# Transformer block with two-of-eight experts on one core: the weight splits of the first sequence spread out, and the experts' bias rows prepared in another way

## What is computed

```python
q, k, v = (xn @ W.T for W in (Wq, Wk, Wv))          # per head
sim = 50 * tanh((q @ k.T) / 8 / 50); sim = where(causal, sim, min)
x = x + (softmax(sim) @ v) @ Wo.T
t = layernorm(x)
shared = gelu(t @ sw1 + sb1) @ sw2 + sb2
probs = softmax(t @ gate_w + gate_b); the two largest -> combine
y[e] = gelu(t @ w1[e] + b1[e]) @ w2[e] + b2[e]
out = x + shared + sum over e of combine[:, e] * y[e]
```

## Time and profile before

| | us |
|---|---|
| median of 3 runs (lowest, highest) | 2082.99 (2081.49, 2083.97) |
| the profiled execution, its own time | 2080.42 |
| its span, first to last instruction | 2078.6 |
| busy: PE, PEld, DVE, ACT, POOL | 1922.9, 1517.5, 1527.5, 1415.6, 1030.0 |

### The profile page before, as it was taken

The page is one execution under the profiler, slowest core; times in us unless marked ns, Lnnn a source line. Parts: engine busy times, 40 slices in busy tenths (PEclk is TensorE's granted clock), DMA queues, the critical chain, the costliest instruction groups (busy, mean ns, idle before and its releaser), DMA issues.

```text
span 2078.6 us, 39943 instructions
## 1 busy us (share of the span) xinstructions
PE 1922.9 (93%) x14653; PEld 1517.5 (73%) x14653; DVE 1527.5 (73%) x2803; ACT 1415.6 (68%) x2170; POOL 1030.0 (50%) x1195
## 2 busy tenths in 40 slices
PE   6799999999999999999999999999999873999998
PEld 4576767676767676767676767676767652999998
DVE  5576878787878787878787878787876885565565
ACT  6677777777777777777777777777777731544444
POOL 3344454545454545454545454545454643444444
PEclk9999999999999999999999999999999995999999
DMA  4000010101010101010101010101010124764664
GB/s 132 1 11 11 11 42 11 42 11 42 11 42 11 42 11 42 11 42 12 41 13 40 14 39 15 38 16 37 16 37 6 37 72 134 232 189 132 196 183 140
DMA packets 73665, 112.51 MB, mean 54 GB/s; under 512 B 9715, under 2 KB 52218, under 8 KB 73476
## 3 DMA queue, kind: packets, MB, share of 16 engines
q1 hardware_dynamic: 58468, 67.86, 11.3%
q0 software_dynamic: 15008, 42.10, 5.4%
HBM read 63.10 MB, written 48.65 MB: 54 GB/s over the span
## 4 chain that ended last, share of the span: by engine, by line
PE 81%; ACT 12%; DVE 5%; issue 2%; DMA 1%; POOL 0%; SPq 0%; POOLq 0%; DVEq 0%
PE bank_o L1239 12%; PE ring L1218 7%; PE ring L1145 6%; PE ring L1151 6%; PE ring L1146 6%; PE ring L1197 6%; PE ring L1223 6%; ACT prob L585 3%; PE acc L1262 3%; PE ring L1204 3%; PE acc L1264 3%; PE acc L1270 3%; ACT prob L591 2%; PE bank_d L1253 2%; PE ring L1404 2%; PE ring L1409 2%
## 5 line engine op out<-in xcount | busy, mean ns | idle before, releaser
L508 POOL TENSOR_SCALAR_AFFINE_SELECT prob<-prob 128x256 f32<-128x256 f32 x512 | 231.1, 473 | 567.7 <-ACT prob L591 567.6
L585 ACT ACTIVATE prob<-ring 128x1024 f32<-128x1024 f32 (+1 forms) x384 | 326.3, 875 | 205.5 <-PE ring L1223 202.3
L591 ACT ACTIVATE prob<-prob 128x1024 f32<-128x1024 f32 (+1 forms) x384 | 342.7, 915 | 5.2
L520 POOL TENSOR_TENSOR key_sum<-prob 128x768 f32<-128x768 f32 x128 | 243.0, 1898 | 205.6 <-PE bank_d L1253 193.9
L1239 PE MATMUL bank_o<-prob,v 128*32 128x512 f32 (+3 forms) x4096 | 306.6, 440 | 25.1 <-DVE weighed L801 14.4
L1218 PE MATMUL ring<-qT,kT 128*128 128x256 f32 (+3 forms) x1024 | 240.2, 336 | 64.7 <-ACT qT L608 20.0
L780 DVE TENSOR_TENSOR kT<-ring,kT 64x512 fp32r<-64x512 f32 x256 | 176.3, 689 | 153.6 <-ACT kT L598 146.8
L1218 PEld LDWEIGHTS ring<-qT,kT 128*128 128x128 f32 x1024 | 166.6, 191 | 146.5 <-issue 71.2
L1239 PEld LDWEIGHTS bank_o<-prob,v 128*32 128x32 f32 x4096 | 118.0, 110 | 185.1 <-issue 159.1
L796 DVE RECIPROCAL norm<-bank_d 128x512 f32<-128x512 f32 x64 | 214.9, 3357 | 21.7 <-PE bank_d L1253 20.1
L1223 PE MATMUL ring<-q_lo,kT 128*128 128x256 f32 (+3 forms) x1024 | 229.6, 326 | 0.9 <-DVE q_lo L785 0.9
(11 more groups left out here) (224 smaller groups left out, 4689.7 us busy)
## 6 DMA issues: line engine op xcount, KB each, us to landing
xin<-first SPq DMA_DIRECT2D x71, 257.0 KB, 3.1
xin<-second SPq DMA_DIRECT2D x71, 129.0 KB, 2.3
xin<-base SPq DMA_DIRECT2D x71, 128.0 KB, 2.5
x_next<-in_x SPq DMA_DIRECT2D x16, 512.0 KB, 4.6
x_res<-in_x SPq DMA_DIRECT2D x16, 512.0 KB, 4.0
raw_e<-in_w SPq DMA_DIRECT2D x4, 1024.0 KB, 6.7
first<-pad SPq DMA_DIRECT2D x9, 257.0 KB, 4.4
second<-pad SPq DMA_DIRECT2D x9, 129.0 KB, 7.5
```

The costliest lines, as they stand in the source:

```text
L508: last = nc.gpsimd.affine_select(out=diag, in_=diag, compare_op=ALU.is_ge, fill=0.0, base=0, pattern=[[0, 2], [1, P]], channel_multiplier=-1)
L520: nc.gpsimd.tensor_tensor(sums[:, :, :], t0[:, :, P:N], t13[:, :, 0:N - P], ALU.add).then_inc(sum_steps, 1)
L585: nc.scalar.activation(probs[p % PROBS][u][:, :, :], slot[:, :, 0:UNIT_COLS[u]], ACT.Tanh, scale=SCALE / SOFTCLAMP).then_inc(act_emptied, 1)
L591: nc.scalar.activation(cols, cols, ACT.Exp, scale=SOFTCLAMP).then_inc(exp_done, 1)
```

## The change

The weight splits of sequence 0 are done at other places and partly on another engine. `w_v` leaves `parts`; POOL makes both of its parts ahead of its loop. Of `w_k` and `w_q` DVE first splits the first 128 columns of each chunk (`split_lo_part`), and the rest after K and Q of pair 0; PE's projection of pair 1 now waits for the rest. `w_o`, `w_1` and `w_2` are split at the end of pairs 2, 3 and 4 (`LATER_SPLIT`), on ACT and on DVE. PE's wait for `w_o` and the constants moves from the end of pair 2 to that of pair 3.

The biases `b1`, `b2` and `sb2` are loaded by one transfer, laid over all 128 partitions (16, 16 and 2 columns each). DVE splits them with two instructions in the opening, and SP, after a wait for them that stands ahead of its loop over the sequences, issues six transfers from SBUF to SBUF that place the high and low parts in their rows. `prepare_bias`, its four loads and the waits for them are gone, as is the work on `sb2` on two partitions. The diff, its repeated declarations left out:

```diff
@@ -177,6 +177,10 @@
         b_rows = sb("b_rows", [P, E * D], F32R)
+        BIAS = E * D // P
+        bias_raw = sb("bias_raw", [P, 2 * BIAS + D // P])
+        bias_part = [sb(f"bias_{s}", [P, 2 * BIAS + D // P], F32R) for s in ("h", "l")]
@@ -322,7 +326,7 @@
         loaded = [sem(f"loaded{k}") for k in range(len(loads))]
-        parts = [("w_k", 0), ("w_q", 1), ("w_v", 2), ("w_o", 3), ("w_1", 5), ("w_2", 6)]
+        parts = [("w_k", 0), ("w_q", 1), ("w_o", 3), ("w_1", 5), ("w_2", 6)]
@@ -332,7 +336,8 @@
         TILE = tile_list()
-        BIAS_STEPS = 5
+        LATER_SPLIT = {2: 2, 3: 3, 4: 4}
@@ -343,29 +348,31 @@
                 if k == 3:
-                    sp.dma_start(sb2_part[0][:, :], sb2_twice).then_inc(small_loaded, 16)
+                    sp.dma_start(bias_raw[:, :], bias_cols).then_inc(small_loaded, 16)
...
             sp.dma_start(base[IDLE_ROW:ROWS, :], pad[:, BASE:]).then_inc(idle_padded, 16)
+            sp.wait_ge(bias_split, 2)
+            sp.wait_ge(const2_ready, 1)
+            for m, part in enumerate(bias_part):
+                for k in range(K):
+                    sp.dma_start(b_rows[k * QD + m:k * QD + m + 1, :].bitcast(F32),
+                                 part[:, k * BIAS:(k + 1) * BIAS].bitcast(F32)).then_inc(bias_placed, 16)
+                sp.dma_start(sb2_rows[m:m + 1, :].bitcast(F32),
+                             part[:, 2 * BIAS:].bitcast(F32)).then_inc(bias_placed, 16)
...
                     sp.dma_start(x_next[:, :, :], x_tiles[i + 1]).then_inc(xnext_loaded, 16)
-                else:
-                    sp.wait_ge(ring_full, AT["turn1", i, 0, 0] + 1)
-                    sp.dma_start(b_raw[0], b1_twice[:, 0:E * D // 2]).then_inc(bias_loaded, 16)
-            for n, (src, half) in enumerate([(b1_twice, 1), (b2_twice, 0), (b2_twice, 1)]):
-                sp.wait_ge(bias_steps, BIAS_STEPS + 4 * (n + 1))
-                at = half * E * D // 2
-                sp.dma_start(b_raw[(n + 1) // 2], src[:, at:at + E * D // 2]).then_inc(bias_loaded, 16)
@@ -526,7 +533,14 @@
+            pool.wait_ge(loaded[2], 16)
+            nc.gpsimd.tensor_copy(split["w_v"][0][:, :], raw["w_v"][:, :]).then_inc(v_split, 1)
+            pool.wait_ge(v_split, 1)
+            nc.gpsimd.tensor_tensor(split["w_v"][1][:, :], raw["w_v"][:, :], split["w_v"][0][:, :].bitcast(F32),
+                                    ALU.subtract).then_inc(v_split, 1)
             pool.wait_ge(const_ready, 2)
+            pool.wait_ge(v_split, 2)
@@ -635,12 +649,9 @@
             copy_qk_hi(0, 0)
-            split_hi(2)
...
                 for p in range(PAIRS):
-                    if i == 0 and p == PROBS - 1:
-                        act.wait_ge(bias_steps, BIAS_STEPS - 1)
@@ -663,8 +674,8 @@
                         exponentiate(i, p, 1)
-                    if i == 0 and p <= 2:
-                        split_hi(3 + p)
+                    if i == 0 and p in LATER_SPLIT:
+                        split_hi(LATER_SPLIT[p])
@@ -721,6 +732,13 @@
                                         split[name][0][:, :].bitcast(F32), ALU.subtract).then_inc(lo_split, 1)
+            def split_lo_part(k, part):
+                name, _ = parts[k]
+                dve.wait_ge(hi_split, k + 1)
+                hi, lo, src = (w[:, :].rearrange("p (c f) -> p c f", c=DC)[:, :, part]
+                               for w in (split[name][0], split[name][1], raw[name]))
+                return nc.vector.tensor_tensor(lo, src, hi.bitcast(F32), ALU.subtract)
@@ -939,43 +957,20 @@
-            split_lo(0)
+            for k in range(2):
+                split_lo_part(k, slice(0, P)).then_inc(lo_first, 1)
...
-            split_lo(1)
...
-            split_lo(2)
+            for k in range(2):
+                split_lo_part(k, slice(P, HD)).then_inc(lo_split, 1)
...
-            dve.wait_ge(const_ready, 2)
-            nc.vector.tensor_copy(sb2_rows[0:K, :], sb2_part[0][:, :]).then_inc(bias_steps, 1)
-            dve.wait_ge(bias_steps, 1)
-            nc.vector.tensor_tensor(sb2_part[0][:, :], sb2_part[0][:, :], sb2_rows[0:K, :].bitcast(F32),
-                                    ALU.subtract).then_inc(bias_steps, 1)
-            dve.wait_ge(bias_steps, 2)
-            nc.vector.tensor_scalar(sb2_part[1][:, :], sb2_rows[0:K, :].bitcast(F32), ident[0:K, 0:1], None,
-                                    ALU.mult).then_inc(bias_steps, 1)
-            dve.wait_ge(bias_steps, 3)
-            nc.vector.scalar_tensor_tensor(sb2_rows[0:K, :], sb2_part[0][:, :], ident[0:K, 1:2],
-                                           sb2_part[1][:, :], ALU.mult, ALU.add).then_inc(bias_steps, 1)
+            nc.vector.tensor_copy(bias_part[0][:, :], bias_raw[:, :]).then_inc(bias_split, 1)
+            dve.wait_ge(bias_split, 1)
+            nc.vector.tensor_tensor(bias_part[1][:, :], bias_raw[:, :], bias_part[0][:, :].bitcast(F32),
+                                    ALU.subtract).then_inc(bias_split, 1)
...
-            nc.vector.tensor_copy(earlier[:, :], earlier_f).then_inc(bias_steps, 1)
-            def prepare_bias(n):
-                k, half = n // 2, slice(n % 2 * E * D // 2, (n % 2 + 1) * E * D // 2)
-                at = slice(k * QD, k * QD + K)
-                row, steps, b = b_rows[at, half], BIAS_STEPS + 4 * n, b_raw[k]
-                pick = [ident[at, k * QD + m:k * QD + m + 1] for m in range(2)]
-                dve.wait_ge(bias_loaded, 16 * (n + 1))
-                nc.vector.tensor_copy(row, b).then_inc(bias_steps, 1)
-                dve.wait_ge(bias_steps, steps + 1)
-                nc.vector.tensor_tensor(b, b, row.bitcast(F32), ALU.subtract).then_inc(bias_steps, 1)
-                dve.wait_ge(bias_steps, steps + 2)
-                nc.vector.tensor_scalar(row, row.bitcast(F32), pick[0], None,
-                                        ALU.mult).then_inc(bias_steps, 1)
-                dve.wait_ge(bias_steps, steps + 3)
-                nc.vector.scalar_tensor_tensor(row, b, pick[1], row.bitcast(F32),
-                                               ALU.mult, ALU.add).then_inc(bias_steps, 1)
+            nc.vector.tensor_copy(earlier[:, :], earlier_f).then_inc(ones_copied, 1)
@@ -1017,10 +1012,6 @@
                         split_values(*chunk)
-                    if i == 0 and p <= 1:
-                        split_lo(3 + p)
-                        if p == 1:
-                            split_lo(5)
@@ -1033,8 +1024,8 @@
                         normalise_rows(i - 1)
-                    if i == NSEQ - 1 and p in (4, 5, 6, 7):
-                        prepare_bias(p - 4)
+                    if i == 0 and p in LATER_SPLIT:
+                        split_lo(LATER_SPLIT[p])
@@ -1327,7 +1318,7 @@
             pe.wait_ge(xn_hi, 1)
-            project_qk(0, 0, (lo_split, 1), (lo_split, 2))
+            project_qk(0, 0, (lo_first, 1), (lo_first, 2))
@@ -1338,7 +1329,9 @@
                         project_out(i - 1, p + 4)
-                    if p + 1 < PAIRS:
+                    if i == 0 and p == 0:
+                        project_qk(0, 1, (lo_split, 1), (lo_split, 2))
+                    elif p + 1 < PAIRS:
@@ -1352,7 +1345,7 @@
                         else:
-                            pe.wait_ge(lo_split, 3)
+                            pe.wait_ge(v_split, 2)
@@ -1364,9 +1357,10 @@
                         denominators(i - 1, PAIRS // 2 - 1)
-                    if i == 0 and p == 2:
-                        pe.wait_ge(lo_split, 4)
-                        pe.wait_ge(bias_steps, BIAS_STEPS)
+                    if i == 0 and p == 3:
+                        pe.wait_ge(lo_split, 3)
+                        pe.wait_ge(ones_copied, 1)
+                        pe.wait_ge(bias_placed, 16 * 6)
@@ -1448,7 +1442,6 @@
             pe.wait_ge(e_lo, 8)
-            pe.wait_ge(bias_steps, BIAS_STEPS + 16)
@@ -1496,9 +1486,7 @@
         "b1s_cols": laid(np.asarray(L0_ffn_sb1).reshape(FC, P).T),
-        "sb2_twice": twice(L0_ffn_sb2),
-        "b1_twice": twice(L0_ffn_b1),
-        "b2_twice": twice(L0_ffn_b2),
+        "bias_cols": laid(np.concatenate([np.asarray(b).reshape(P, -1) for b in (L0_ffn_b1, L0_ffn_b2, L0_ffn_sb2)], 1)),
```

More of the change, by code:

```diff
@@ L119, in block_program @@
 def block_program(nc, x, wqT, wkT, wvT, woT, gate_w, gate_b_rows, w1s, w1, w2s, w2,
-                  b1s_cols, sb2_twice, b1_twice, b2_twice, out):
+                  b1s_cols, bias_cols, out):
     first = nc.dram_tensor("first", (ROWS, FIRST_ROW), F32).ap()
@@ L230, in block_program @@
             pad = sb("pad", [P, ROW], F32, arena)
-            sb2_part = [sb(f"sb2_{s}", [K, D], F32, arena) for s in ("raw", "part")]
         head_rows = [slice(0, DH), slice(DH, P)]
-        b_raw = [x_next[at:at + K, :, :].rearrange("p t d -> p (t d)") for at in (0, QD)]
         earlier_f = norm[:, 0:P]
@@ L247, in block_program @@
         lo_split = sem("lo_split")
+        v_split = sem("v_split")
         const_ready = sem("const_ready")
@@ L282, in block_program @@
         e_lo = sem("e_lo")
```

(8 more changed lines are left out.)

## The result

| | before | after |
|---|---|---|
| median of 4 runs each (lowest, highest), us | 2083.14 (2081.49, 2083.97) | 2067.56 (2063.09, 2068.45) |
| ratio, 95% interval | | 0.9922, 0.9905 to 0.9939 |
| profiled execution, its span | 2080.42, 2078.6 | 2068.23, 2066.5 |

The kernel is 15.6 us faster, where I had forecast 26.3, and 1.1 us above my range. The page's busy line shows that DVE lost 20.9 us of work (most of it the bias work). It also shows what nobody asked for: PE executes as many instructions as before, 14653, and is busy 5.6 us longer than the 1922.9 of before.

What follows compares the result with a forecast made beforehand. PE, busy nearly everywhere, was taken to wait for DVE results in sequences 0 and 15. Opening 12.5 + last sequence 13.8 = 26.3 off 2080.4 gave 2054.1; 2.6 added gave 2056.7, range 2051 to 2066.5.

Steps and rivals of the forecast that it cites:

- The change touches nothing in there: Steady sequences between 1 and 14: period stays 103.80 us, so the change's worth lies only in sequences 0 and 15.
- The big wait: Opening, DVE's 14.14 us wait before sequence 1's norm: goes, norm hidden, pair 3's scores at 63.4 against 74.01, shift 10.6.
- w_o off pair 0: Opening, ACT's 1.88 us cast before pair 1's tanh: PE's whole 1.76 us wait goes, and 1.6 of slow clock at pair 2.
- w_o at pair 2: Opening, w_o's 1.88 us cast ahead of the last V copy: shift falls by 1.3 to 2.7, `values` at 60.2.
- w_v on GpSimd: Opening, w_v split on POOL: copy 4.0 us (between 1.79 and 4.8), 9 with the subtraction; costs nothing.
- My rule against the change: Opening: two-input DVE work and POOL exclude each other, so w_v's subtraction could delay the rest of K; at most 0.5 lost.
- the meeting with POOL: Last sequence, fourth burst: POOL's last sums now meet DVE's low part of `oT`, taking 0.8 off shift 13.4.
- The clock term of 1.2: Last sequence, `values` of pair 6 and denominators: wait falls from 4.02 to about 2.6, winning 1.2 of 1.35 us.
- A: Rival, opening: SP's six issues stall like the 4.87 us one, x_next late, 9.7 us lost, time 2066.4; chance 0.10.
- C: Rival, opening: each of six transfers holds SP's queue over 7.6 us; kernel slower (at 10 us each: 2097); chance 0.03.
- B: Rival, last sequence: bias bursts were mostly cover, only about 8.5 us won and no clock, time 2062; chance 0.12.
- D: Rival, opening: w_v or the masks on POOL are late; needs 25 us where 9 was forecast; inside the range.

Runs made afterwards that it cites:

- the version with both mends: The change with 32 unused bytes behind the bias tiles and ACT's last V copy ahead of w_o's cast; 2057.99 us, ratio 0.9862.
- the norm's run: The kernel before, with the low parts of w_1 and w_2 made on DVE behind the norm of sequence 1; 2074.94 us, ratio 0.9946.

## Why the prediction was wrong

**The step that failed** is "The change touches nothing in there", with "From there to the end nothing changes". I read the instruction streams and left out where the tiles stand. 480 bytes cost 14 x 0.40 = 5.6 us in the sequences and 142 x 0.0138 = 2.0 in the experts; the medians say 7.5 with the change and 7.1 (2092.73 - 2085.67) with 480 idle bytes. Without this term the time would have been near 2060 to 2063, inside the range and 3 to 6 above the forecast. "Wrong if the steady period changes" was the right alarm.

**The opening, 12.5 forecast, 9.4 measured.** The big wait: right; the norm ran at 41.9, was hidden, and PE went from denominators to scores. `values` at 60.2: it came at 60.75. What I mis-sized is what follows. I took 3.2 us from `values` to the end of the denominators and scores at 63.4. The wait before it had grown from 2.38 to 3.65, the clock fell, and the scores came at 66.6. That was no accident: after 3.65 the 32 products were at the low level, for the most part at least, in all four profiles that have this wait (3.68 to 4.50 us), after 2.4 at the high one in all ten (2.36). I had counted this clock cost at two other places and not behind the wait that my own term made longer. w_o off pair 0 (1.8, and 1.6 of clock): the gap there did go, and the first V product came 3.9 earlier (42.55 to 38.67), as forecast. But ten profiles of the old order reach it anywhere from 38.8 to 42.9, and the run with w_o back was no slower, so this price rested on one draw of the clock and the term pays nothing net. From there w_o at pair 2 took back 1.8 (I took 1.3, the low end). w_v on GpSimd: no cost, as said; its cast took 1.89, so of my two bounds (1.79 and 4.8) the one I rejected was right. My rule against the change found nothing to hold: the subtraction ended at 19.4 and the rest of K began at 21.7. That DVE and POOL hold each other up did show elsewhere: with w_o's low part gone from beside it, POOL's 512-column add took 1.28 instead of 3.22. The first columns: Q's products started without a wait, worth half a microsecond at most.

**The last sequence, 13.8 forecast, 11.7 measured at the last reciprocal.** Taking off the shift of 3.7 that came with it, `values` of pair 5 gained 1689.75 - 1676.88 - 3.7 = 9.1 (forecast 9.4) and those of pair 6 11.6 (12.6). One cost is the meeting with POOL that I had allowed 0.8: beside POOL's sums `oTh` took 1.41 and `oTl` behind it 1.11, where they take 0.43 and 0.69 alone, 1.4 in all. The Trainium skill, SBUF — State Buffer, "Who interferes with whom", lists casts among the DVE operations that can contend with GpSimd for the port pair that they share. The trace fits: both outlast a sum of POOL's that began just before them. The clock term of 1.2 did not come: the wait fell to 2.7 as forecast, and the products still ran at the low level, 3.99 and 3.53. In the run with the V copy first the same wait of 2.72 was followed by 2.36, but in the seven other profiles with the new bias rows by 3.57 to 4.03. So this term is a chance, and a small one. The whole sequence varies: from its first to its last reciprocal it took 64.8 to 69.2 us in these eight profiles, and 78.4 to 79.8 in the nine with the old rows.

**The rivals.** A and C, the queue: refuted by six issues of 0.6 us. The long issue stayed with the one load behind the weights (5.55, it was 4.87). B, the bursts as cover: refuted by the bias rows' half alone: from the first to the last reciprocal of sequence 15 it takes 66.8 us instead of 78.4, 11.6 less, where B left 8.5. Even the longest of the eight against the shortest of the nine is 9.2 less. D: w_v was ready 19 us before it was wanted.

## What to carry to other kernels

A new tile, however small, moves all tiles behind it. When a change that should touch one stage alters a steady period elsewhere, compare PE's busy time over equal work, then pad the new tiles (here a multiple of 256 bytes cost nothing) and look again. And before work is moved to another engine, try to move what waits behind it: the order of one norm and two small subtractions gained 12.1 us, about as much as the whole new opening (11.2).

## What was not expected of the hardware

**TensorE's products take longer depending on where an operand starts.** Five of the six groups of 512-column K and Q products went from 391 to 392 ns to 395 to 399 with `xnT` 32 bytes off, at a granted clock of 1.00 in both. The stretches of eight steady sequences, before and then with xnT alone moved:

```profile
451.86:1282.27 830.41, 797.82 (x6050) 600.63 (x6049) 653.51 (x1161) 625.87 (x865) 435.69 (x513) 1.00 0.08 27
```

```profile
453.38:1286.61 833.23, 801.17 (x6050) 600.41 (x6049) 653.82 (x1161) 626.07 (x865) 434.61 (x513) 1.00 0.08 26
```

The counts agree, and DVE, ACT and POOL are as busy as before. The Trainium skill, SBUF — State Buffer, "Who interferes with whom", says that PE never waits on anyone. By that rule the loss is no wait for another engine, and the equal busy times agree; PE still loses 0.4% here. Why stays open: whether the absolute address counts or its distance to that of the weights (they never moved), and what happens at other shifts than the ones tried.

**The clock is partly a matter of chance.** Before `values` of pair 2, waits of 1.86 us were followed by the low level once (4.05) and by the high one twice (2.36, also in the version with both mends). At the start the same projection products reached 0.39 us at about 17 us in the norm's run and at 28 us in the kernel before, on unchanged code, and by the first V product the two were 3.7 us apart. One profile can't price a gap of 2 to 3 us.
